# GGN layer of a four-layer graph network: node table as three bf16 pieces, one bf16 matmul of 384 columns per edge tile in place of an f32 one

## The chip, the core and the metric

The kernel runs on one core of one Trainium2 chip. The metric is the device time of one execution in microseconds (us). A core has five engines that run side by side and meet only at semaphores: PE (matmuls; its weight loads are listed as PEld), DVE (vector), ACT (scalar), POOL and SP; DMA queues move data between HBM and on-chip memory. POOL also issues the gathers: indirect DMAs that fetch one table row for each of 128 edges.

## The reference

6250 nodes with 128 features and 100000 edges, sorted by destination, pass four layers: a GAT with two rounds, a GCN, a relational attention layer, and a gated graph layer (GGN). After each, `x = layernorm(x + layer(x))`. The change touches the last layer only:

```python
h = x @ W_in.T + b_in
m = h @ W_msg
agg = jax.ops.segment_sum(m[src], dst, num_segments=n_nodes)
gi = agg @ W_ih.T + b_ih
gh = h @ W_hh.T + b_hh
i_r, i_z, i_n = jnp.split(gi, 3, axis=-1)
h_r, h_z, h_n = jnp.split(gh, 3, axis=-1)
r = jax.nn.sigmoid(i_r + h_r)
z = jax.nn.sigmoid(i_z + h_z)
n = jnp.tanh(i_n + r * h_n)
h_new = (1.0 - z) * n + z * h
return h_new @ W_out.T + b_out
```

The destinations are not spread evenly: an edge's destination is 6250 times the square of a uniform number, so the first blocks of nodes hold the most edges.

## The kernel before, in words

Nodes stand in 49 blocks of 128 (`BLOCKS`), padded to 52 and handled four at a time: 13 quads (`QUADS`). Edges stand in 196 groups (`GROUPS`) of 512, each of four tiles (`GT`) of 128 edges. A visit is one group against one block of destinations; there are 196 + 49 - 1 = 244 visits (`V`), since a group that crosses a block's border is visited again. The whole program is one stage after another, with a barrier between them. Three stages matter here.

**The table stage** (`norm_nodes`, called with the name `ggnt`) takes the sums of the layer ahead, applies the layernorm and writes the table of messages `m` to HBM (`ggn_tab`). It is a pipeline over quads. In turn q of its loop DVE does: the input sums of quad q (L1800, four of L1804), the negative mean (L1702), the reciprocal and offset of quad q-1 (L1705, L1707), and the take of quad q-3 (L1821, in `ggn_take`: the product in PSUM plus a bias, to `ggnt_gsb`). ACT does in its turn q: the squares of quad q (four of L1726, which wait for the mean of quad q), the square root (L1729), and the copy of the transposed quad q-2 (L1734). POOL normalizes a quad (L1744) once its offset is there, PE transposes it (L1755) and multiplies quad q-1 (L1763), SP stores each quad that was taken (L1776). Every engine keeps its own program order.

**The edge stage** (`ggn_edges`) sums table rows by destination. POOL gathers four tiles of 128 rows per group (L265, `gather_group`) into a ring of 14 groups (`SLOTS`), and waits for a slot until PE has made the last visit to the group that lay there (the semaphore `s_o`). SP counts the groups that have landed. DVE makes for each visit four one-hot tiles (L1871, from `iota` and the edge's destination in its block). PE does for each visit four matmuls into one of two PSUM banks (L1954: one-hot times rows; each f32 matmul stands in the trace as two records), after waiting, at every fourth visit, for the group of the visit three ahead. DVE adds the bank to the block's sums (L1879). DVE's order is: one-hots of visit v+1, then the sum of visit v. Ahead of the visits PE and ACT compute `h` and a part of the gates for the 13 quads (L1930, L1937, L1943).

**The gates** (`ggn_gates`) and the last layernorm follow.

The relational layer's table stage (the same `norm_nodes`, under the name `reln`) already cuts a result into three bf16 pieces in `rel_take_dve` and `rel_take_act`: a copy on ACT (L2371), then on DVE a difference (L2378), a cast (L2380) and a difference (L2382). There the pieces of a quad are made one turn late, behind the next quad's take.

## Time and profile before

| what | us |
|---|---|
| three timed runs | 5886.95, 5890.31, 5895.29 |
| their median | 5890.31 |
| span of the profiled execution, first to last instruction | 6933.2 |
| span less median | 1042.9 |

Only the span is shown for the profiled execution; no time of its own around it stands beside it. Its span is 1042.9 us longer than the median of the timed runs, so a difference of two stages in the profile isn't by itself a difference in the time.

A row of a group reads: line, engine, operation, written tile <- read tiles, shapes, count | busy us, mean ns of one | idle time of the engine ahead of them, and what ended most of it. "issue" is a gap in which the engine waited for nothing that the trace shows. In a timeline a row is: start us, duration us, engine, line, operation, tiles, count, and in brackets the idle time before it.

### The profile page before, as it was taken

The page shows a single profiled execution, that of the slowest core. Times are in us where ns is not written, and L with a number is a line of the kernel's source. Part 1 is how long each engine was busy: PE and PEld are TensorE (multiplying, and loading weights), DVE is VectorE, ACT ScalarE, POOL GpSimd, SP SyncE. Part 2 cuts the span into 40 slices and gives each one's busy share as a digit, 9 for nine tenths or more (in the row PEclk, how much of TensorE's full clock was granted, in tenths as well). Part 3 has the DMA queues.
Part 4 walks back from the last instruction along what each step waited for, and adds up shares of the span by engine and source line. Part 5 has one row for each costly group of instructions (what it writes and reads, how often), then busy time and mean ns, then how long its engine had stood idle before and what let it go on. Part 6 is the DMA issues. An engine that isn't in the chain of part 4 may idle for free. (4 is left out here: it accounts for less than half of the span.)

```text
span 6933.2 us, 103287 instructions
## 1 busy us (share of the span) xinstructions
PE 3719.0 (54%) x29332; PEld 3188.5 (46%) x29332; DVE 3593.0 (52%) x11040; ACT 1531.5 (22%) x3908; POOL 3988.6 (58%) x4360
## 2 busy tenths in 40 slices
PE   3555466555434452434454588888885853333436
PEld 1444355544333442334444477777774742223334
DVE  3278655587723343333344577777778951122225
ACT  0255200255300002000000244444442130000003
POOL 6366666266666645666666366666661455666662
PEclk8655577855566676555555799999997976566568
DMA  5266433366522223555564255555553731111111
GB/s 159 88 195 197 141 107 109 95 194 195 165 71 74 73 68 89 137 145 150 157 164 128 72 174 174 175 173 176 174 175 96 205 87 40 47 45 46 45 45 33
DMA packets 511394, 846.13 MB, mean 122 GB/s; under 512 B 116566, under 2 KB 220655, under 8 KB 510271
## 3 DMA queue, kind: packets, MB, share of 16 engines
q0 software_dynamic: 140576, 316.92, 17.7%
q1 hardware_dynamic: 210451, 305.33, 14.5%
q10 hardware_dynamic: 159840, 217.27, 10.8%
q8 instruction: 279, 4.57, 0.3%
q14 instruction: 248, 2.03, 0.1%
HBM read 654.62 MB, written 186.50 MB: 121 GB/s over the span
## 5 line engine op out<-in xcount | busy, mean ns | idle before, releaser
L2456 POOL DMA_INDIRECT s_rows<-rel_tab,src_v x832 | 786.6, 945 | 489.9 <-remote 280.7
L265 POOL DMA_INDIRECT stash<-gat_tab,src_g x784 | 750.9, 958 | 424.3 <-issue 167.4
L265 POOL DMA_INDIRECT gcn_rows<-gcn_tab,src_g x784 | 754.6, 963 | 416.2 <-issue 227.1
L265 POOL DMA_INDIRECT ggn_rows<-ggn_tab,src_g x784 | 744.2, 949 | 413.7 <-issue 224.8
L1621 PE MATMUL e_psb<-tmp,e_oh 128*128 x3328 | 639.7, 362 | 602.0 <-DVE e_oh L1589 391.1
L265 POOL DMA_INDIRECT stash<-in_x,src_g x732 | 705.8, 964 | 385.3 <-issue 154.6
L1621 PEld LDWEIGHTS e_psb<-tmp,e_oh 128*128 128x128 f32 x3328 | 575.2, 262 | 666.9 <-issue 666.4
L1954 PE MATMUL ggn_pso<-ggn_rows,ggn_oh 128*128 x1952 | 389.0, 374 | 693.1 <-issue 273.0
L1169 PE MATMUL g_psc<-g_parts,g_oh 128*128 128x52 bf16 x9408 | 480.5, 222 | 479.5 <-DVE g_oh L1088 260.7
L1954 PEld LDWEIGHTS ggn_pso<-ggn_rows,ggn_oh 128*128 128x128 f32 x1952 | 351.8, 274 | 731.0 <-issue 729.3
L1169 PEld LDWEIGHTS g_psc<-g_parts,g_oh 128*128 128x128 bf16 x9408 | 426.3, 120 | 534.3 <-DVE g_oh L1088 294.6
L2127 PE MATMUL gcn_pso<-gcn_rows,gcn_oh 128*128 x1952 | 452.9, 407 | 153.7 <-issue 84.6
L1879 DVE TENSOR_TENSOR acc<-acc,ggn_pso 128x128 f32 x244 | 70.0, 287 | 895.8 <-DMA tmp<-typev_rows 660.6
L2127 PEld LDWEIGHTS gcn_pso<-gcn_rows,gcn_oh 128*128 128x128 f32 x1952 | 393.8, 300 | 172.9 <-issue 168.7
L2067 DVE TENSOR_TENSOR acc<-acc,gcn_pso 128x128 f32 x244 | 69.8, 286 | 740.9 <-DMA g_lo_rows<-lo_rows 585.9
L1586 DVE COPY tmp<-gx 128x12 f32<-128x12 f32 x392 | 70.5, 180 | 661.3 <-DMA p_early_edges<-in_src 304.0
L2138 PE MATMUL pre_psr<-vt_nv_pieces,tmp 128*128 x832 | 92.5, 182 | 525.5 <-DVE tmp L2080 351.8
L1061 ACT ACTIVATE acc<-g_lo_rows,g_neg_pid 128x512 f32<-128x512 bf16 x392 | 282.9, 722 | 403.3 <-DVE g_oh L1088 225.5
L2138 PEld LDWEIGHTS pre_psr<-vt_nv_pieces,tmp 128*128 128x128 bf16 x832 | 81.2, 114 | 564.1 <-issue 549.6
L1101 DVE TENSOR_TENSOR g_eq<-g_eq,g_psc 128x416 f32<-128x416 f32 x392 | 228.8, 584 | 193.3 <-PE g_psc L1169 144.2
L2485 DVE TENSOR_TENSOR s_psr<-s_psr,s_rows 128x512 f32<-128x512 f32 x208 | 144.8, 696 | 350.2 <-ACT s_psr L2610 301.5
L2610 ACT ACTIVATE s_psr<-s_psr,tm_v 128x128 f32<-128x128 f32 x832 | 230.0, 338 | 417.1 <-remote 379.0
(507 smaller groups left out, 8609.8 us busy)
## 6 DMA issues: line engine op xcount, KB each, us to landing
g_lo_rows<-lo_rows ACTq DMA_DIRECT2D x392, 256.0 KB
oh_dram<-tmp ACTq DMA_DIRECT2D x208, 256.0 KB
s_oh<-oh_dram SPq DMA_DIRECT2D x208, 256.0 KB
edge_v<-acc SPq DMA_DIRECT2D x208, 256.0 KB
r_values<-edge_v SPq DMA_DIRECT2D x208, 256.0 KB, 2.9
edge_v<-stash SPq DMA_DIRECT2D x205, 256.0 KB
e_values<-edge_v SPq DMA_DIRECT2D x205, 256.0 KB
tmp<-drel_rows ACTq DMA_DIRECT2D x208, 128.0 KB
```

Source lines behind the costliest of these rows:

```text
L265: pool.indirect_dma_start(rows[:, t, :], None, tab[:, :], bass.IndirectOffsetOnAxis(ap=edges[:, t:t + 1], axis=0)).then_inc(s_land, 16)
L1061: nc.scalar.activation(sq[:, k % 2, :], trow[:, k, GE:2 * GE], ACT.Square, bias=neg_pid[:, :]).then_inc(s_sq, 1)
L1101: v.tensor_tensor(eq[:, k % 2, :, :, :], eq[:, k % 2, :, :, :], cand, ALU.mult).then_inc(s_take, 1)
L1169: m = nc.tensor.matmul(ps_c[k % 2][:, a * GT + t, 0:NBP], oh[:, k, a * GE + t * P:a * GE + (t + 1) * P], part[:, a, n, :], start=(n == 0), ...
L1586: v.tensor_copy(wv4[:, k, :, D:WCOLS], w.rearrange("p h t -> p t h"))
L1621: nc.tensor.matmul(ps_b[:, bass.ds(bank, 1), 0:WCOLS].rearrange("p o d -> p (o d)"), oh[:, k, t, :], wv[:, bass.ds(slot, 1), :].rearrange( ...
L1954: m = nc.tensor.matmul(ps_o[k % 2][:, 0:D], oh[:, k % 2, t, :], rows[:, bass.ds(slots[k], 1), t, :].rearrange("p o d -> p (o d)"), start=( ...
L2127: m = mm(ps_o[k % 2][:, 0:D], oh[:, k % 2, t, :], rows[:, bass.ds(slots[k], 1), t, :].rearrange("p o d -> p (o d)"), start=(t == 0), stop= ...
L2138: m = mm(ps_n[k % 2][:, t, :], oh2[:, k, t * P:(t + 1) * P], nvp[:, bass.ds(b, 1), :].rearrange("p o n -> p (o n)"), start=True, stop=True)
L2456: pool.indirect_dma_start(rows[:, n % RING, t, :], None, rel_tab[:, :], bass.IndirectOffsetOnAxis(ap=src_v[:, n * GT + t:n * GT + t + 1], ...
L2485: v.tensor_tensor(hm, hm, rows[:, s, :, D:2 * D], ALU.add).then_inc(s_h, 1)
L2610: m = f(ps_r[h][:, t, D:2 * D], ps_r[h][:, t, D:2 * D], ACT.Copy, scale=tm_v[:, bass.ds(n * GT + t, 1)])
```

## The change

The table gets 384 bf16 columns in place of 128 f32 ones: each value is stored as a bf16 number, the bf16 of what is left, and the bf16 of what is then left. A row grows from 512 to 768 bytes. One-hots become bf16, and a tile's sum is one bf16 matmul with 384 columns. DVE adds the three parts of the bank one after another. In the table stage the take of a quad now makes the pieces: DVE adds the bias, ACT copies the first piece, DVE subtracts it, casts the second and subtracts for the third. `w_tab`, `drel_v`, `src_v` and `tm_v` are given back earlier, which makes room for the wider ring; nothing else of the program moves.

```diff
-        ggn_tab = nc.dram_tensor("ggn_tab", (NPAD, D), F32).ap()
+        ggn_tab = nc.dram_tensor("ggn_tab", (NPAD, 3 * D), BF16).ap()
...
+        def ggn_piece(q, i):
+            return pieces[:, q % 2, :, i * D:(i + 1) * D]
+
+        def ggn_take_act(act, q, s_ch, s_eva):
+            act.wait_ge(s_ch, q + 1)
+            nc.scalar.activation(ggn_piece(q, 0), g_rest[:, q % 2, :, :], ACT.Copy).then_inc(s_eva, 1)
+
         def ggn_take(dve, v, q, ps_c, gsb, s_eva, s_ch):
-            return v.tensor_tensor(gsb, ps_c[:, :, 0:D], bias_ggn[:, :].unsqueeze(1).to_broadcast([P, 4, D]), ALU.add)
+            r = g_rest[:, q % 2, :, :]
+            v.tensor_tensor(r, ps_c[:, :, 0:D], bias_ggn[:, :].unsqueeze(1).to_broadcast([P, 4, D]), ALU.add).then_inc(s_ch, 1)
+            if q == 0:
+                v.tensor_copy(iota16[:, :], iota[:, :])
+            dve.wait_ge(s_eva, q + 1)
+            v.tensor_tensor(r, r, ggn_piece(q, 0), ALU.subtract).then_inc(s_gp, 1)
+            dve.wait_ge(s_gp, 2 * q + 1)
+            v.tensor_copy(ggn_piece(q, 1), r).then_inc(s_gp, 1)
+            dve.wait_ge(s_gp, 2 * q + 2)
+            return v.tensor_tensor(ggn_piece(q, 2), r, ggn_piece(q, 1), ALU.subtract)
...
-                rows = sb(st, f"ggn_rows", [P, SLOTS, GT, D])
-                oh = sb(st, f"ggn_oh", [P, 2, GT, P])
+                rows = sb(st, f"ggn_rows", [P, SLOTS, GT, 3 * D], BF16)
+                oh = sb(st, f"ggn_oh", [P, 2, GT, P], BF16)
...
-                                i = v_.tensor_scalar(oh[:, k % 2, t, :], iota[:, :], dst_tab[:, col_], None, ALU.is_equal)
+                                i = v_.tensor_scalar(oh[:, k % 2, t, :], iota16[:, :], dst_tab[:, col_], None, ALU.is_equal)
...
-                            dve.wait_ge(s_acc, v + 2)
                             dve.wait_ge(s_o, v + 1 + RING)
                             ab = acc[:, bass.ds(b * D, D)]
-                            v_.tensor_tensor(ab, ab, ps_o[k % 2][:, 0:D], ALU.add).then_inc(s_acc, 1)
+                            for n in range(3):
+                                dve.wait_ge(s_acc, 3 * v + n + 2)
+                                v_.tensor_tensor(ab, ab, ps_o[k % 2][:, n * D:(n + 1) * D], ALU.add).then_inc(s_acc, 1)
...
-                                pe.wait_ge(s_acc, v + 1)
+                                if v >= 2:
+                                    pe.wait_ge(s_acc, 3 * (v - 1) + 2)
                                 for t in range(GT):
-                                    m = nc.tensor.matmul(ps_o[k % 2][:, 0:D], oh[:, k % 2, t, :], rows[:, bass.ds(slots[k], 1), t, :].rearrange("p o d -> p (o d)"),
+                                    m = nc.tensor.matmul(ps_o[k % 2][:, 0:3 * D], oh[:, k % 2, t, :], rows[:, bass.ds(slots[k], 1), t, :].rearrange("p o d -> p (o d)"),
                                                          start=(t == 0), stop=(t == GT - 1))
...
-        norm_nodes("ggnt", rel_in, w_ggn[:, :], D, [(ggn_tab, None)], None, ggn_take, rel_begin)
+            norm_nodes("ggnt", rel_in, w_ggn[:, :], D, [(ggn_tab, "pieces")], ggn_take_act, ggn_take, rel_begin)
```

On DVE, in the middle of the table stage, one turn of the loop stands in the kernel before like this (input sums, mean, reciprocal, offset, take):

```order
7107 L1800 TENSOR_TENSOR acc<-acc,zrel 128x512
7108 L1804 SCALAR_TENSOR_TENSOR x_n,ggnt_sum<-acc,x_n 128x128 x4
7109 L1702 TENSOR_SCALAR ggnt_minus_mean<-ggnt_sum 128x4
7110 L1705 RECIPROCAL ggnt_sd<-ggnt_sd 128x4
7111 L1707 TENSOR_TENSOR ggnt_off<-ggnt_minus_mean,ggnt_sd 128x4
7112 L1821 TENSOR_TENSOR ggnt_gsb<-ggnt_psc,bias_ggn 128x512
```

and in the changed one like this:

```order
7120 L1805 TENSOR_TENSOR acc<-acc,zrel 128x512
7121 L1809 SCALAR_TENSOR_TENSOR x_n,ggnt_sum<-acc,x_n 128x128 x4
7122 L1704 TENSOR_SCALAR ggnt_minus_mean<-ggnt_sum 128x4
7123 L1707 RECIPROCAL ggnt_sd<-ggnt_sd 128x4
7124 L1709 TENSOR_TENSOR ggnt_off<-ggnt_minus_mean,ggnt_sd 128x4
7125 L1834 TENSOR_TENSOR g_rest<-ggnt_psc,bias_ggn 128x512
7126 L1838 TENSOR_TENSOR g_rest<-g_rest,g_pieces 128x512
7127 L1840 CAST g_pieces<-g_rest 128x4x128
7128 L1842 TENSOR_TENSOR g_pieces<-g_rest,g_pieces 128x4x128
```

The take is now four operations in a row, and the first difference (L1838) reads what ACT has written; the next quad's input sums stand behind all of them.

On ACT the same turn is, in the changed kernel (squares, root, copy of the transposed quad, and the new first piece):

```order
4071 L1728 ACTIVATE ggnt_junk,ggnt_var<-x_n,ggnt_minus_mean 128x128 x4
4072 L1731 ACTIVATE ggnt_sd<-ggnt_var,eps_c 128x4
4073 L1736 ACTIVATE ggnt_xT<-ggnt_psa 128x512
4074 L1830 ACTIVATE g_pieces<-g_rest 128x4x128
4075 L1728 ACTIVATE ggnt_junk,ggnt_var<-x_n,ggnt_minus_mean 128x128 x4
```

The new copy (L1830) stands last in the turn, behind the four squares, which wait for the mean that DVE wrote in this same turn.

In the edge stage DVE's row for one visit (block number, sum, the next one-hots) was in the kernel before:

```order
7560 L1875 TENSOR_LOAD blk_row
7561 L1875 ISA x2
7562 L1879 ISA
7563 L1879 TENSOR_TENSOR acc<-acc,ggn_pso 128x128
7564 L1871 TENSOR_SCALAR ggn_oh<-iota,dst_tab 128x128 x4
```

and is now:

```order
7567 L1896 TENSOR_LOAD blk_row
7568 L1896 ISA x2
7569 L1901 ISA
7570 L1901 TENSOR_TENSOR acc<-acc,ggn_pso 128x128 x3
7571 L1892 TENSOR_SCALAR ggn_oh<-iota,dst_tab 128x128 x4
```

One sum became three; the one-hots keep their place and count.

## Rows read from the trace of the kernel before

**Rows 1.** The page, costliest groups: the five large gathers of the program.

```profile
L2456 POOL DMA_INDIRECT s_rows<-rel_tab,src_v x832 | 786.6, 945 | 489.9 <-remote 280.7
L265 POOL DMA_INDIRECT stash<-gat_tab,src_g x784 | 750.9, 958 | 424.3 <-issue 167.4
L265 POOL DMA_INDIRECT gcn_rows<-gcn_tab,src_g x784 | 754.6, 963 | 416.2 <-issue 227.1
L265 POOL DMA_INDIRECT ggn_rows<-ggn_tab,src_g x784 | 744.2, 949 | 413.7 <-issue 224.8
L265 POOL DMA_INDIRECT stash<-in_x,src_g x732 | 705.8, 964 | 385.3 <-issue 154.6
```

**Rows 2.** Instructions on the ring `ggn_rows`: ns min/median/max, first and last start.

```profile
L1954 PE MATMUL ggn_pso<-ggn_rows,ggn_oh x1952: 274/421/578, 5751.8 to 6833.3; 128*128 x196
L265 POOL DMA_INDIRECT ggn_rows<-ggn_tab,src_g x784: 938/944/1325, 5660.2 to 6809.0; - x196
```

**Rows 3.** Timeline inside the edge stage: POOL's gathers, and one wait of POOL and DVE.

```profile
5783.10 0.94 POOL L265 DMA_INDIRECT ggn_rows<-ggn_tab,src_g  x1 [0.31 <-issue]
5784.35 0.94 POOL L265 DMA_INDIRECT ggn_rows<-ggn_tab,src_g  x1 [0.30 <-issue]
5787.82 0.29 DVE L1879 TENSOR_TENSOR acc<-acc,ggn_pso 128x128 f32 x1 [6.71 <-DMA tmp<-typev_rows]
5788.39 0.94 POOL L265 DMA_INDIRECT ggn_rows<-ggn_tab,src_g  x1 [3.09 <-DMA tmp<-typev_rows]
```

**Rows 4.** Busy time by stretch of 100 us (PE, PEld, DVE, ACT, POOL; PEclk, DMA share, GB/s).

```profile
6460.00:6560.00 100.00, 42.74 (x192) 37.95 (x192) 30.01 (x126) 0.00 (x0) 65.36 (x68) 0.58 0.18 45
```

**Rows 5.** Timeline of DVE, the last visits of the edge stage.

```profile
6830.19 0.29 DVE L1879 TENSOR_TENSOR acc<-acc,ggn_pso 128x128 f32 x1 [0.67 <-PE ggn_pso L1954]
6830.39 0.87 DVE L1871 TENSOR_SCALAR ggn_oh<-iota,dst_tab 128x128 f32<-128x128 f32 x4
6831.18 0.28 DVE L1879 TENSOR_TENSOR acc<-acc,ggn_pso 128x128 f32 x1
...
6832.77 0.29 DVE L1879 TENSOR_TENSOR acc<-acc,ggn_pso 128x128 f32 x1 [0.53 <-PE ggn_pso L1954]
```

**Rows 6.** The takes of the table stage: ns min/median/max, first and last start, waits.

```profile
L1821 DVE TENSOR_TENSOR ggnt_gsb<-ggnt_psc,bias_ggn x13: 684/692/692, 5612.4 to 5655.5; 128x512 f32<-128x512 f32 x13
...
  PE ggnt_psc L1763: 16.9, 8
```

**Rows 7.** Timeline of DVE in the table stage: first take, and means of quads 4 and 12.

```profile
5612.42 0.69 DVE L1821 TENSOR_TENSOR ggnt_gsb<-ggnt_psc,bias_ggn 128x512 f32<-128x512 f32 x1 [2.91 <-PE ggnt_psc L1763]
5613.03 0.68 DVE L1800 TENSOR_TENSOR acc<-acc,zrel 128x512 f32<-128x512 f32 x1
...
5614.71 0.17 DVE L1702 TENSOR_SCALAR ggnt_minus_mean<-ggnt_sum 128x4 f32<-128x4 f32 x1
...
5647.62 0.17 DVE L1702 TENSOR_SCALAR ggnt_minus_mean<-ggnt_sum 128x4 f32<-128x4 f32 x1
...
5650.05 0.16 DVE L1707 TENSOR_TENSOR ggnt_off<-ggnt_minus_mean,ggnt_sd 128x4 f32<-128x4 f32 x1
...
5654.55 0.69 DVE L1821 TENSOR_TENSOR ggnt_gsb<-ggnt_psc,bias_ggn 128x512 f32<-128x512 f32 x1 [1.53 <-PE ggnt_psc L1763]
```

**Rows 8.** Timeline of DVE in the `reln` table stage: the pieces of one quad.

```profile
3904.38 0.68 DVE L2378 TENSOR_TENSOR q_rest<-q_rest,acc 128x512 f32<-128x512 f32 x1
3905.09 0.43 DVE L2380 CAST tmp<-q_rest 128x512 bf16<-128x512 f32 x1
3905.55 0.69 DVE L2382 TENSOR_TENSOR tmp<-q_rest,tmp 128x512 bf16<-128x512 f32 x1
3906.16 0.68 DVE L2392 TENSOR_TENSOR reln_gsb<-reln_psc,w_b 128x512 f32<-128x512 f32 x1
```

**Rows 9.** The next turn there: DVE's mean, then ACT's squares to first piece.

```profile
3907.97 0.17 DVE L1702 TENSOR_SCALAR reln_minus_mean<-reln_sum 128x4 f32<-128x4 f32 x1
3908.17 0.40 ACT L1726 ACTIVATE reln_junk<-x_n,reln_minus_mean 128x128 f32<-128x128 f32 x1 [3.05 <-DVE reln_minus_mean L1702]
...
3910.53 0.62 ACT L2371 ACTIVATE acc<-q_rest 128x512 bf16<-128x512 f32 x1
```

**Rows 10.** The page: time from issue to landing of a table store, the last number.

```profile
ggn_tab<-ggnt_gsb SPq DMA_DIRECT2D x13, 256.0 KB, 2.3
```

**Rows 11.** Groups of one shape: bf16 operations elsewhere in the program.

```profile
L2079 DVE TENSOR_SCALAR tmp<-tmp,vt_pid 128x512 bf16<-128x512 bf16 x208 | 75.3, 362 | 1.8 <-DMA tmp<-typev_rows 1.0 <-issue 0.8
L2546 PE MATMUL s_psr<-rel_hm,s_oh 128*128 128x256 bf16 x832 | 195.6, 275 | 16.8 <-DMA s_oh<-oh_dram 12.8 <-issue 3.9
L2574 PE MATMUL s_psk<-bkp,ones 128*128 128x512 bf16 x208 | 79.3, 381 | 38.2 <-issue 33.0 <-DVE tmp L2510 5.2
```

More of the change, by code:

```diff
@@ L126, in build @@
         iota = sb(top, "iota", [P, P])
+        iota16 = sb(top, "iota16", [P, P], BF16)
         x_n = sb(top, "x_n", [P, NBP * D])
@@ L130, in build @@
         dst_tab = sb(top, "dst_tab", [P, VP * GT])
-        w_tab = sb(top, "w_tab", [P, VP * GT])
         blk_row = sb(top, "blk_row", [1, VP], I32)
@@ L138, in build @@
         done_row = sb(top, "done_row", [1, GROUPS], I32)
-        drel_v = sb(top, "drel_v", [P, VT])
-        src_v = sb(top, "src_v", [P, VT], I32)
-        tm_v = sb(top, "tm_v", [P, VT])
         blkv_row = sb(top, "blkv_row", [1, VT], I32)
@@ L286, in keep_rows @@
                 keep_store(sp, l, j)
+        visits = ExitStack()
+        w_tab = sb(visits, "w_tab", [P, VP * GT])
+        drel_v = sb(visits, "drel_v", [P, VT])
+        src_v = sb(visits, "src_v", [P, VT], I32)
+        tm_v = sb(visits, "tm_v", [P, VT])
         gat = ExitStack()
@@ L1774, in _ @@
                             for tab, source in stores:
-                                src = gsb[:, q % 2, :, :] if source is None else qd(source, q).rearrange("p (j d) -> p j d", d=D)
+                                if source == "pieces":
+                                    src = pieces[:, q % 2, :, :]
+                                else:
+                                    src = gsb[:, q % 2, :, :] if source is None else qd(source, q).rearrange("p (j d) -> p j d", d=D)
                                 sp.dma_start(tab[q * 4 * P:(q + 1) * 4 * P, :].rearrange("(j p) c -> p j c", p=P), src).then_inc(s_st[q % 2], 16)
@@ L1902, in _ @@
                         back(V - 1, (V - 1) % RING)
-                        dve.wait_ge(s_acc, V + 2)
+                        dve.wait_ge(s_acc, 3 * V + 2)
                     @block.scalar
@@ L2783, in build @@
         rel_sums()
-        norm_nodes("ggnt", rel_in, w_ggn[:, :], D, [(ggn_tab, None)], None, ggn_take, rel_begin)
+        with ExitStack() as spare:
+            g_rest = sb(spare, "g_rest", [P, 2, 4, D])
+            pieces = sb(spare, "g_pieces", [P, 2, 4, 3 * D], BF16)
+            s_gp = top.enter_context(nc.semaphore("g_pieces_made"))
+            norm_nodes("ggnt", rel_in, w_ggn[:, :], D, [(ggn_tab, "pieces")], ggn_take_act, ggn_take, rel_begin)
         rel.close()
+        visits.close()
         hb = sb(top, "ggn_candidate", [P, NBP * D])
```

## The prediction

> **What bounds the kernel now.** I read the page's costliest groups first. The five large gathers [rows 1] look alike: a gather takes POOL 945 to 964 ns, and an idle time stands beside it in the same proportion everywhere. The timeline shows how this comes about [rows 3]: gathers start 1.25 us apart (0.94 us of work, 0.30 us of gap), and now and then POOL stops for some us and goes on together with DVE, on an event that the trace doesn't show. In the edge stage of the GGN the 784 gathers run from 5660.2 to 6809.0 [rows 2], and the stage's matmuls end 25 us later. At their own pace they would need 784 x 1.247 = 978 us; they took 1150.
>
> Who then sets the pace of that stage? Not PE: its 192 records in 100 us are 24 visits (8 records each), and they keep it busy 43 us; DVE is busy 30 us, while POOL issues 68 gathers, 17 groups, and is busy 65 us [rows 4]. With a gap of 0.30 us per gather that is 85 us of POOL's 100. So POOL is the engine at work, and PE and DVE follow it.
>
> The missing 15% are the joint stops. They matter, because the profiled span is 1042.9 us longer than the median of the timed runs. Taking 0.31 us per gather off the idle times of [rows 1] leaves 232, 181, 173, 171 and 158 us, together 915 us. That is close to the whole difference, so I take it that timed runs gather at about 1.247 us without the stops, and that the edge stage lasts there some 978 us plus its last visits. This is an inference; a rival below lives on its being wrong.
>
> The table stage ahead of it is bound otherwise. Its 13 takes go from 5612.4 to 5655.5, DVE waiting only 16.9 us for PE in it [rows 6]: DVE, ACT, POOL and PE hand each quad around, with nothing large that could cover an added step, and the gathers can't begin before its last store has landed.
>
> **The change part by part.**
>
> *PE in the edge stage.* A matmul of 384 bf16 columns lies between the bf16 ones of 256 (275 ns) and 512 columns (381 ns) [rows 11], by interpolation 328 ns, against two records of 421 ns (median) [rows 2]. Records of a stream overlap, so I take about 1.3 us for four of them, where a visit's eight records took 1.1 to 2.1 us. PE has 4.0 us per visit (978 / 244). Worth nothing on the path.
>
> *Gathers.* A row grows from 512 to 768 bytes. The relational gathers fetch 1024-byte rows at 945 ns against 949 here [rows 1], so issuing doesn't depend on the row's size. The DMA engines are busy 18% [rows 4]; half as many bytes again makes some 27%. Zero.
>
> *DVE in the edge stage.* Unhindered, a visit costs DVE 0.99 us, from one sum to the next [rows 5]. Two sums are added. Each waits for the one before: at least 0.29 us, and with a semaphore between (0.71 us start to start for a 0.68 us operation, [rows 8]) 0.33 us; at most 0.5 us, the sum's 0.29 us plus the 0.2 us by which any next operation follows it here. One-hots get cheaper: 512 bf16 columns take 362 ns [rows 11], where four of 128 f32 columns take 0.87 us, so between nothing and 0.5 us. A visit then costs 1.15 to 2.0 us; I take 1.9, since the four short one-hots stay four instructions. In the busiest part there are 24 visits to 17 groups, 1.4 a group, so 2.7 us of DVE in the 5.0 us that POOL needs for a group. Hidden by the gathers. Were that cover gone, 244 x 0.9 = 220 us would show.
>
> *Last visits.* Behind the last landing there are four visits. Before they go in pairs of 2.6 us at the fast clock (6830.19 to 6832.77, [rows 5]) and slower at the other, the first two starting at once: about 8.5 us. After, DVE's 1.9 us rules: 1.5 + 4 x 1.6 to 1.9, about 8 us. I put -0.6, with +-3.
>
> *The table stage.* This is the term that counts. ACT's new copy stands behind the four squares of the same turn, and these wait for the mean that DVE has just written; DVE then stands still until the copy is there, makes the pieces, and only then begins the next quad's sums, on which the next mean depends. So the turn becomes a closed loop through both engines:
> - from DVE's mean to the end of ACT's copy: 3910.53 + 0.62 - 3907.97 = 3.18 us, and about 0.1 us to reach DVE [rows 9];
> - difference, cast, difference, until the next operation starts: 3906.16 - 3904.38 = 1.78 us [rows 8];
> - the next quad's input sums until its mean: 5614.71 - 5613.03 = 1.68 us [rows 7].
>
> That makes 6.74, with hand-overs 6.8 us a turn. Now eight turns, from the mean of quad 4 to that of quad 12, take 5647.62 - 5614.71 = 32.9 us [rows 7], 4.1 each; then they take 54.4: **+21.5 us**. In the turn of the first take ACT is free: bias add 0.69, copy 0.62, pieces 1.78 and the small cast of `iota` come to 3.3 us until the next sums instead of 0.61: **+2.7**. Behind the mean of quad 12 the stage needs 5655.5 + 0.7 - 5647.6 = 8.5 us now [rows 6, 7]. Then: 5.1 for the take of quad 9; 0.35 to the offset of quad 12; 4.5 from an offset to the product one quad back (5650.05 to 5654.55, [rows 7]), which covers the take of quad 10; and two takes of 3.2 us for quads 11 and 12. Together 16.3: **+7.8**. Sum of the stage: **+32.0 us**.
>
> Bounds: the DVE work alone is 13 x 1.78 = 23.1 us, and if it filled DVE's 16.9 us of waits [rows 6] it would cost 6; if no part of a turn overlapped with anything it would cost 13 x (3.3 + 1.78) = 66. The loop's hand-overs leave +-5 around 32.
>
> *Stores.* 384 KB a quad in place of 256, landing 2.3 us after issue [rows 10]. Only the last counts: 0 to +1.2 (in proportion), +0.6 taken. Room in memory and the released tables: nothing.
>
> Sum: 32.0 + 0.6 - 0.6 = **+32 us**. Against the profiled execution that is 6933.2 + 32 = 6965 if the joint stops stay as they are; against the timed median, 5890.3 + 32 = **5922 us**.
>
> Two rules of the Trainium skill bear on this. The page "SBUF — State Buffer", section "Who interferes with whom", says that a VectorE cast or tensor-scalar operation in a two-port mode keeps GpSimd off the port pair that it also uses to write its DMA descriptors, for the whole instruction. By that rule shorter one-hots would free the gathers; the row bounds it: mean 949 ns against a median of 944, so 784 x 5 ns = 4 us at most, and the sum would be +28. The other, "VectorE: DVE Perf Modes", section "The DRAIN you can't avoid", says that each VectorE operation pays its own pipeline flush, chained or not, and so speaks against three sums in place of one; the sums are priced above from rows and lie hidden.
>
> **The rivals.**
>
> *A. The stops are partly real in timed runs, and the change relieves them: faster.* For it: POOL and DVE restart together on something that hangs on PE [rows 3], and PE's records fall by half. Against it: the 915 us. If 40% of this stage's 171 us were real and went away, the time would be 32 - 68 = -36: 5854 us. It decides from 45 us of stops removed in timed runs. 0.10.
>
> *B. The pieces fill waits in the table stage: no change that can be measured.* 23.1 - 16.9 = +6: 5896 us. For it: DVE waits every other turn now. Against it: ACT's program order puts the copy behind the squares of the same turn. It needs the copy to be ready about when the bias add is done. 0.11.
>
> *C. DVE falls behind in the edge stage: much slower.* It needs a visit of over 3.5 us in the busy part (5.0 / 1.4), or a backlog like that of the profile at the end: 25 us of visits at 1.3 us would be 36 at 1.9, so +11 on top, 5933; fully bound by DVE, over 6000. Against it: 1.9 us. 0.03 for the large one.
>
> The forecast itself: 0.76, its own range 5911 to 5934.
>
> **How the numbers follow.** A measurement of this kernel tells changes over about 0.2%, 12 us. Faster is A, 0.10; same is B with a little of the forecast's lower edge, 0.12; slower 0.78. The range leaves out A and the large C and takes in B and the smaller backlog of C: 5895 to 5942.
>
> **What would show it.** In the changed trace: takes about 6.8 us apart in the middle of the table stage, 13 of them from first to last start over some 72 us instead of 43; DVE waiting there for ACT's copy, some 2 us a turn; gathers still 1.25 us apart; PE's busy time in the edge stage well below 389 us. A stage between 48 and 55 us would be B. POOL waiting for PE and DVE's sums with no stop of the joint kind, or over 3.5 us between sums in a burst, would be C. The profiled span itself may even fall, if the stops of a profiled run shrink with the number of records; a fall there together with slower timed runs would bear out the reading of the 1042.9 us, and timed runs that are faster would make it wrong.

## The result, and the profile after

| | us |
|---|---|
| before, median of 4 runs (lowest to highest) | 5892.8 (5887.0 to 5897.3) |
| after, median of 4 runs (lowest to highest) | 5920.9 (5920.1 to 5924.6) |
| after : before, 95% interval | 1.0053 [1.0039, 1.0067] |
| span of the profiled execution of after | 5919.9 |

The changed kernel is 0.5% slower: 28.1 us by these medians, where 32 were predicted. Its profiled span agrees with its timed runs to 1 us. The stops of [rows 3] are gone, and not from the changed stage alone.

The page of the changed kernel, the groups that answer to [rows 1]:

```profile
L2479 POOL DMA_INDIRECT s_rows<-rel_tab,src_v x832 | 787.6, 947 | 271.0 <-issue 252.6
...
L262 POOL DMA_INDIRECT ggn_rows<-ggn_tab,src_g x784 | 745.0, 950 | 252.9 <-issue 234.9
...
L262 POOL DMA_INDIRECT stash<-in_x,src_g x732 | 708.6, 968 | 223.7 <-issue 146.1
```

A gather costs what it did. Four of the five stages of [rows 1] were not touched, and their idle times fell as well (489.9 to 271.0 for the first), so the stops say nothing about the change.

Instructions on the ring `ggn_rows`, answering to [rows 2], with what POOL's gathers waited for and the landing time:

```profile
L1977 PE MATMUL ggn_pso<-ggn_rows,ggn_oh x976: 326/524/528, 4854.8 to 5817.0; 128*128 x196
L262 POOL DMA_INDIRECT ggn_rows<-ggn_tab,src_g x784: 942/947/1462, 4824.8 to 5807.4; - x196
...
  POOL ggn_rows L262: 3.7, 12
DMA to landing us min/median/max: 2.5/2.6/4.1
```

The gathers go from 4824.8 to 5807.4, 1.255 us apart on average, and in the whole stage POOL waited 3.7 us for PE. Rows of 768 bytes land in 2.6 us. The stretch that answers to [rows 4]:

```profile
5460.00:5560.00 100.00, 30.13 (x97) 12.18 (x98) 41.38 (x183) 0.00 (x0) 75.93 (x80) 0.59 0.28 78
```

POOL issues 80 gathers in these 100 us and is the engine at work; PE is busy 30 us, DVE 41. The DMA engines are busy 28%, where 27 were expected.

The takes of the table stage, answering to [rows 6]:

```profile
L1834 DVE TENSOR_TENSOR g_rest<-ggnt_psc,bias_ggn x13: 683/691/693, 4744.3 to 4816.6; 128x512 f32<-128x512 f32 x13
...
  PE ggnt_psc L1765: 4.8, 2
```

They take 72.3 us from first to last start, where [rows 6] had 43.1. One turn, first on DVE and then on ACT:

```profile
4762.60 0.17 DVE L1704 TENSOR_SCALAR ggnt_minus_mean<-ggnt_sum 128x4 f32<-128x4 f32 x1
...
4762.96 0.69 DVE L1834 TENSOR_TENSOR g_rest<-ggnt_psc,bias_ggn 128x512 f32<-128x512 f32 x1
4765.81 0.69 DVE L1838 TENSOR_TENSOR g_rest<-g_rest,g_pieces 128x512 f32<-128x512 f32 x1 [2.16 <-ACT g_pieces L1830]
4766.54 0.43 DVE L1840 CAST g_pieces<-g_rest 128x512 bf16<-128x512 f32 x1
4767.00 0.69 DVE L1842 TENSOR_TENSOR g_pieces<-g_rest,g_pieces 128x512 bf16<-128x512 f32 x1
4767.61 0.68 DVE L1805 TENSOR_TENSOR acc<-acc,zrel 128x512 f32<-128x512 f32 x1
...
4769.30 0.17 DVE L1704 TENSOR_SCALAR ggnt_minus_mean<-ggnt_sum 128x4 f32<-128x4 f32 x1
```

```profile
4762.80 0.40 ACT L1728 ACTIVATE ggnt_junk<-x_n,ggnt_minus_mean 128x128 f32<-128x128 f32 x1 [3.72 <-DVE ggnt_minus_mean L1704]
...
4764.68 0.58 ACT L1736 ACTIVATE ggnt_xT<-ggnt_psa 128x512 f32<-128x512 f32 x1
4765.16 0.62 ACT L1830 ACTIVATE g_pieces<-g_rest 128x512 bf16<-128x512 f32 x1
```

The bias add ends at 4763.65, but ACT is in the squares, which it began after the mean of 4762.60; the root and the copy to `xT` follow, and the first piece is ready only at 4765.78. DVE stands still for 2.16 us and the turn is 6.70 us. The loop's parts are 3.2 us from the mean to the first difference, 1.80 for the pieces and 1.69 for the next quad's sums.

The last visits, on DVE, answering to [rows 5]:

```profile
5813.27 0.93 DVE L1901 TENSOR_TENSOR acc<-acc,ggn_pso 128x128 f32 x3 [9.88 <-PE ggn_pso L1977]
5814.12 0.73 DVE L1892 TENSOR_SCALAR ggn_oh<-iota,dst_tab 128x128 bf16<-128x128 bf16 x4
5814.77 0.92 DVE L1901 TENSOR_TENSOR acc<-acc,ggn_pso 128x128 f32 x3
5815.61 0.73 DVE L1892 TENSOR_SCALAR ggn_oh<-iota,dst_tab 128x128 bf16<-128x128 bf16 x4
5816.26 0.92 DVE L1901 TENSOR_TENSOR acc<-acc,ggn_pso 128x128 f32 x3
```

An unhindered visit is 1.49 us: 0.85 us from the first of three sums to the one-hots, 0.65 from these to the next sum.

### The profile page after: what moved, and what is told of

Same layout as the page of the kernel before. It is cut to its first block and busy times, and to the rows that moved or that the text cites. A ratio compares the mean times of both kernels' runs of the same rounds, so it can differ in the third digit from the quotient of the medians.

```text
span 5919.9 us, 101771 instructions
## 1 busy us (share of the span) xinstructions
PE 3354.0 (57%) x28252; PEld 2842.6 (48%) x28356; DVE 3708.7 (63%) x11568; ACT 1541.7 (26%) x3921; POOL 3989.9 (67%) x4360
## 5 line engine op out<-in xcount | busy, mean ns | idle before, releaser
L2479 POOL DMA_INDIRECT s_rows<-rel_tab,src_v x832 | 787.6, 947 | 271.0 <-issue 252.6
L262 POOL DMA_INDIRECT ggn_rows<-ggn_tab,src_g x784 | 745.0, 950 | 252.9 <-issue 234.9
L2150 PE MATMUL gcn_pso<-gcn_rows,gcn_oh 128*128 x1952 | 407.1, 378 | 532.4 <-SPq L972 521.1
L1977 PE MATMUL ggn_pso<-ggn_rows,ggn_oh 128*128 x976 | 300.4, 466 | 662.5 <-SPq L972 604.0
L2150 PEld LDWEIGHTS gcn_pso<-gcn_rows,gcn_oh 128*128 128x128 f32 x1952 | 356.7, 275 | 549.2 <-issue 548.0
L1901 DVE TENSOR_TENSOR acc<-acc,ggn_pso 128x128 f32 x732 | 208.9, 285 | 619.4 <-PE ggn_pso L1977 601.6
L1977 PEld LDWEIGHTS ggn_pso<-ggn_rows,ggn_oh 128*128 128x128 bf16 x976 | 121.1, 124 | 842.3 <-issue 824.4
L1591 DVE TENSOR_TENSOR e_oh<-e_psi,drel_v 128x512 f32<-128x512 f32 x416 | 284.0, 683 | 22.3 <-PE e_psb L1623 22.3
L2724 POOL COPY r_wv<-score 128x32 f32<-128x32 f32 x208 | 107.9, 519 | 267.6 <-PE r_psb L2768 158.6
L1636 ACT ACTIVATE acc<-e_psb 128x128 f32<-128x128 f32 x98 | 27.2, 278 | 989.9 <-PE e_psb L1623 989.9
L2599 PE MATMUL s_psk<-w_kv,s_msgT 128*128 128x128 f32 x1664 | 219.7, 275 | 110.8 <-DVE tmp L2533 110.5
L2082 DVE TENSOR_SCALAR gcn_oh<-iota,dst_tab,w_tab 128x128 f32<-128x128 f32 x976 | 274.9, 363 | 0.0
```

What stands on the lines that cost most here:

```text
L262: pool.indirect_dma_start(rows[:, t, :], None, tab[:, :], bass.IndirectOffsetOnAxis(ap=edges[:, t:t + 1], axis=0)).then_inc(s_land, 16)
L1591: v.tensor_tensor(oh[:, k % RING, :, :], iota_p.unsqueeze(1).to_broadcast([P, GT, P]), drel_v[:, bass.ds(n * GT, GT)].unsqueeze(2).to_broa ...
L1901: v_.tensor_tensor(ab, ab, ps_o[k % 2][:, n * D:(n + 1) * D], ALU.add).then_inc(s_acc, 1)
L1977: m = nc.tensor.matmul(ps_o[k % 2][:, 0:3 * D], oh[:, k % 2, t, :], rows[:, bass.ds(slots[k], 1), t, :].rearrange("p o d -> p (o d)"), sta ...
L2082: i = v.tensor_scalar(oh[:, k % 2, t, :], iota[:, :], dst_tab[:, col_], w_tab[:, col_], ALU.is_equal, ALU.mult)
L2150: m = mm(ps_o[k % 2][:, 0:D], oh[:, k % 2, t, :], rows[:, bass.ds(slots[k], 1), t, :].rearrange("p o d -> p (o d)"), start=(t == 0), stop= ...
```

## The experiments

Each kernel was timed beside the kernel before on the same chip, but the sets of runs stand on different chips, so two experiments are compared by what each lies above its own runs of before, and by their traces. The changed kernel lies 28.1 us above before in the first set of runs and 35.5 in the second, which is told at the end of this section. "Stage" below is the time from the table stage's first mean to the first gather, read from the trace.

### The kernel before, once more

No edit.

> The kernel before, unchanged, profiled once more. Theory (the joint stops belonged to that one profiled execution and not to the kernel): the new profile has a span within 10 us of the timed runs, about 5890 us, the 784 gathers of the GGN's edge stage start 1.25 us apart and the stage takes about 980 us instead of 1150, and the 13 takes of the table stage still go over some 43 us. Rival (the kernel of before has the stops whenever it is profiled, and the change took them away): a span of some 6930 us again, with gathers' idle time near 490 us.

Measured: 5886.6 us against 5885.9, ratio 1.0002 [0.9993, 1.0011]; the profiled span is 5881.4 us. Its page, and the instructions on the ring and the takes:

```profile
L265 POOL DMA_INDIRECT ggn_rows<-ggn_tab,src_g x784 | 744.0, 949 | 246.8 <-issue 233.1
```

```profile
L265 POOL DMA_INDIRECT ggn_rows<-ggn_tab,src_g x784: 940/944/1351, 4789.5 to 5771.2; - x196
```

```profile
L1821 DVE TENSOR_TENSOR ggnt_gsb<-ggnt_psc,bias_ggn x13: 682/691/692, 4742.1 to 4784.8; 128x512 f32<-128x512 f32 x13
```

The same kernel, without the stops: 246.8 us of idle time before this stage's gathers instead of 413.7, and 1229 instead of 2129 before all five groups of [rows 1]; gathers over 981.7 us instead of 1149, takes over 42.7. The 1042.9 us of the first profile belonged to that one execution. From here on this profile stands for before.

### The edge stage alone, and the table stage alone

In the first, two pieces stay zero, so that it computes with a table rounded to bf16; ACT has no part in the take:

```diff
-            r = g_rest[:, q % 2, :, :]
-            v.tensor_tensor(r, ps_c[:, :, 0:D], bias_ggn[:, :].unsqueeze(1).to_broadcast([P, 4, D]), ALU.add).then_inc(s_ch, 1)
             if q == 0:
                 v.tensor_copy(iota16[:, :], iota[:, :])
...
-            return v.tensor_tensor(ggn_piece(q, 2), r, ggn_piece(q, 1), ALU.subtract)
+                v.memset(pieces[:, :, :, D:3 * D], 0.0)
+            return v.tensor_tensor(ggn_piece(q, 0), ps_c[:, :, 0:D], bias_ggn[:, :].unsqueeze(1).to_broadcast([P, 4, D]), ALU.add)
```

> The edge stage of the change alone: the table is stored as bf16 rows of 384, but the table stage writes only the first piece (one add that writes bf16) and leaves the other two at zero, so the sums are those of a table rounded to bf16. Theory (all of the loss is in the table stage, the edge stage is bound by the gathers' issue in both kernels): within 0.1% of before, 5887 to 5895 us; first to last take about 43 us. Rival 1 (the edge stage gains a little, which hides part of a larger loss): 5880 to 5886. Rival 2 (the two extra sums or the larger rows cost something in the edge stage): over 5897, up to 5920 if the loss is there.

Measured: 5888.6 us against 5885.9, ratio 1.0000 [0.9991, 1.0009]. The takes cover 43.8 us.

The second is the kernel before, with the pieces made beside its f32 table:

```diff
-            return v.tensor_tensor(gsb, ps_c[:, :, 0:D], bias_ggn[:, :].unsqueeze(1).to_broadcast([P, 4, D]), ALU.add)
...
+            v.tensor_tensor(s, ps_c[:, :, 0:D], bias_ggn[:, :].unsqueeze(1).to_broadcast([P, 4, D]), ALU.add).then_inc(s_ch, 1)
+            if q == 0:
+                v.tensor_copy(iota16[:, :], iota[:, :])
+            dve.wait_ge(s_eva, q + 1)
+            v.tensor_tensor(r, s, ggn_piece(q, 0), ALU.subtract).then_inc(s_gp, 1)
+            dve.wait_ge(s_gp, 2 * q + 1)
+            v.tensor_copy(ggn_piece(q, 1), r).then_inc(s_gp, 1)
+            dve.wait_ge(s_gp, 2 * q + 2)
+            return v.tensor_tensor(ggn_piece(q, 2), r, ggn_piece(q, 1), ALU.subtract)
```

> The table stage of the change alone: the three pieces are made as in the change, by the same operations and waits, but the f32 table is stored and the f32 edge stage of before follows; the pieces are used by nobody. Theory: the whole loss appears, 5917 to 5926 us, with turns of 6.7 us and 13 takes over 72 us. Rival (the loss is in the edge stage): within 3 us of before, 5890.

Measured: 5917.1 us against 5885.9, ratio 1.0051 [1.0037, 1.0065]. The takes of this kernel:

```profile
L1833 DVE TENSOR_TENSOR g_sum<-ggnt_psc,bias_ggn x13: 683/691/693, 4744.7 to 4817.0; 128x512 f32<-128x512 f32 x13
```

72.3 us again. The two halves of the change add up to the whole: from the edge stage nothing that the timed runs can tell (their interval is 5 us to either side), 31 us from the table stage.

### Pieces made one turn later

```diff
+                            if q >= 4 and late is not None:
+                                late(dve, v, q - 4, s_eva)
                             if q >= 3:
                                 dve.wait_ge(s_mm, q - 2)
...
-                            sp.wait_ge(s_evd, q + 1)
+                            if late is None:
+                                sp.wait_ge(s_evd, q + 1)
+                            else:
+                                sp.wait_ge(s_gp, 3 * (q + 1))
```

> The changed kernel with one thing moved: a quad's two differences and the cast are made one turn later, after the next offset, so that DVE no longer waits for ACT's copy of the same turn. Same operations, same edge stage. Theory (the turn of 6.7 us is a closed loop through ACT's squares and copy): the turn becomes DVE's own work, 1.7 (sums and mean) + 0.4 (reciprocal, offset) + 1.8 (pieces) + 0.7 (bias add) = 4.6 to 4.9 us, eight turns give back 14 to 17 us and the tail 1 to 4: 5901 to 5907 us. Rival (the added DVE work itself is what costs, not the waiting): DVE's work is the same, so 5917 to 5923.

Measured: 5899.6 us against 5885.9, ratio 1.0024 [1.0014, 1.0035]. It lies 13.7 us above before, where the changed kernel lies 28 to 36 above it and the pieces alone 31.2 on this same chip: 14 to 22 us of the loss are given back. By the traces it is 18.7, and the time is a little better than expected. One turn on DVE, and POOL beside it:

```profile
4763.52 0.17 DVE L1704 TENSOR_SCALAR ggnt_minus_mean<-ggnt_sum 128x4 f32<-128x4 f32 x1
...
4763.89 0.68 DVE L1852 TENSOR_TENSOR g_rest<-g_rest,g_pieces 128x512 f32<-128x512 f32 x1
4764.61 0.57 DVE L1854 CAST g_pieces<-g_rest 128x512 bf16<-128x512 f32 x1
4765.21 0.82 DVE L1856 TENSOR_TENSOR g_pieces<-g_rest,g_pieces 128x512 bf16<-128x512 f32 x1
4765.95 0.68 DVE L1844 TENSOR_TENSOR g_rest<-ggnt_psc,bias_ggn 128x512 f32<-128x512 f32 x1
4766.55 0.76 DVE L1813 TENSOR_TENSOR acc<-acc,zrel 128x512 f32<-128x512 f32 x1
...
4768.32 0.17 DVE L1704 TENSOR_SCALAR ggnt_minus_mean<-ggnt_sum 128x4 f32<-128x4 f32 x1
```

```profile
4764.07 2.71 POOL L1751 TENSOR_SCALAR x_n<-x_n,ggnt_sd,ggnt_off 128x128 f32<-128x128 f32 x4 [2.09 <-DVE ggnt_off L1709]
```

No wait is left on DVE in these turns, and the turn is 4.80 us, DVE's own work. So 1.9 us of the 2.6 us that each turn had gained were waiting and 0.7 us are work; of these 0.7 us, 0.27 are the cast and the last difference, which take longer beside POOL's scaling than in the changed kernel (0.57 and 0.82 us instead of 0.43 and 0.69). From the mean of quad 4 to that of quad 12 it takes 38.5 us instead of 53.6 (before: 32.5), and the whole stage 72.7 instead of 91.4 (before: 59.3). The tail gave back only 1.0 us, the low end of what was expected: with no sums left to stand between, each of the last takes still waits for its own copy (0.69 to 0.70 us, as in the changed kernel's tail below).

### ACT's copy ahead of its squares

```diff
+                            first = name == "ggnt" and 3 <= q < QUADS
+                            if first:
+                                take_act(act, q - 3, s_ch, s_eva)
                             if q < QUADS:
                                 act.wait_ge(s_nm, q + 1)
```

> The changed kernel with ACT's order changed in the table stage alone: from the fourth turn to the thirteenth the copy of the first piece stands ahead of the four squares, not behind them. Theory (DVE's wait of 2.2 us a turn is for squares that stand ahead of the copy): the copy is there about 0.7 us after the bias add, the turn becomes 1.7 + 0.4 + 0.7 + 0.7 + 1.8 = 5.3 us, ten turns of which eight in full give back 11 to 14 us: 5907 to 5910 us. Rival (the squares, moved behind, hold up reciprocal and offset, and the loop is as long as before by another way round): turn 6.3 to 6.8, 5917 to 5923 us.

> The kernel with ACT's copy ahead of the squares, once more, on the chip of the changed kernel. Its first profile has turns of 5.87 us and takes over 64.9 us in place of 72.3, but its timed median lay only 3.6 us below that of the changed kernel, in another set of runs. Theory (turns of 0.83 us less, 7 us in all, are real): 6 to 9 us below the changed kernel's median here. Rival (nothing is gained in timed runs): within 3 us of it.

Measured: 5917.3 us against 5888.2 (ratio 1.0052 [1.0038, 1.0065]), and the second time 5912.8 us beside 5920.6 of the changed kernel on the same chip (ratio 1.0048 [1.0035, 1.0062] to 5885.1). The gain is about half of what was first expected: a turn is 5.87 us, not 5.3. The 6 to 9 us expected of the second run came as 7.8. DVE in the first of the two profiles:

```profile
4765.08 0.69 DVE L1837 TENSOR_TENSOR g_rest<-ggnt_psc,bias_ggn 128x512 f32<-128x512 f32 x1 [0.56 <-PE ggnt_psc L1768]
4766.47 0.69 DVE L1841 TENSOR_TENSOR g_rest<-g_rest,g_pieces 128x512 f32<-128x512 f32 x1 [0.70 <-ACT g_pieces L1833]
```

The wait for the copy fell from 2.16 to 0.70 us as expected, but a new one of 0.56 us stands before the bias add. ACT's squares, and behind them its copy of `xT`, are now later, and PE's product with them. What stands ahead of the copy on ACT (the squares, the root and the copy of `xT`) is thus shown to be what DVE waits for; moving it only shortens the loop from 6.70 to 5.87 us. The second profile has a stage of 85.2 us against 91.4, 6.2 us less. In the first set of runs the timings show no gain (29.0 us above its own before, where the changed kernel was 28.1 above its own); on one chip all five runs (5911.9 to 5918.3 us) lie below the five of the changed kernel (5918.9 to 5924.0). The intervals of the ratios, 8 us to either side, could not tell the gain from none; the traces can.

### The first piece cast on DVE

```diff
+            dve.wait_ge(s_ch, q + 1)
+            v.tensor_copy(ggn_piece(q, 0), r).then_inc(s_eva, 1)
             dve.wait_ge(s_eva, q + 1)
```

> The changed kernel with the first piece cast by DVE itself in place of ACT's copy: one more DVE operation a turn, and no hand-over to ACT and back. Theory (the waiting costs, 2.2 us a turn; the cast costs 0.4 to 0.6): turn 4.9 to 5.2 us, 12 to 15 us given back in eight turns and 0 to 3 at the end: 5903 to 5909 us. Rival (DVE's own work bounds the turn): DVE has more of it, so 5925 us or more.

Measured: 5912.7 us against 5888.2, ratio 1.0044 [1.0030, 1.0058]. More work on DVE, and yet not slower than the changed kernel: its turns are 5.3 and 5.8 us by turns, 5.51 on average. The rival is out, but the gain is smaller than expected: eight turns give back 9.5 us where 12 to 15 were expected, the stage 11.4 (80.0 instead of 91.4), and by what each lies above its own before it is 4 to 11. In each turn two of DVE's four operations on the pieces were longer than the ones they were priced by, and these lie beside POOL's scaling (4763.21 to 4765.83 in this turn):

```profile
4764.94 0.57 DVE L1842 CAST g_pieces<-g_rest 128x512 bf16<-128x512 f32 x1
4765.54 0.82 DVE L1844 TENSOR_TENSOR g_pieces<-g_rest,g_pieces 128x512 bf16<-128x512 f32 x1
```

0.57 and 0.82 us, where the same two take 0.43 and 0.69 in the changed kernel.

### More sums in the edge stage

Nine and twelve chained sums a visit instead of three; those past the third go to a tile that nothing reads.

```diff
-                            for n in range(3):
-                                dve.wait_ge(s_acc, 3 * v + n + 2)
-                                v_.tensor_tensor(ab, ab, ps_o[k % 2][:, n * D:(n + 1) * D], ALU.add).then_inc(s_acc, 1)
+                            for n in range(9):
+                                dve.wait_ge(s_acc, 9 * v + n + 2)
+                                to = ab if n < 3 else more[:, :]
+                                v_.tensor_tensor(to, to, ps_o[k % 2][:, n % 3 * D:(n % 3 + 1) * D], ALU.add).then_inc(s_acc, 1)
```

> The changed kernel with nine chained sums a visit instead of three in the edge stage; the six added ones go to a tile that nobody reads. Nothing else is changed. Theory (DVE's sums lie hidden under the issue of the gathers): a visit costs DVE 1.5 + 6 x 0.32 = 3.4 us where the gathers give 4.0, so the stage stays at 984 us, and only the four visits behind the last gather show, 4 x 1.9 = 8 us: 5927 to 5933 us, with a few us more if bursts of visits overrun. Rival (sums are on the path, the two added ones too): 244 x 1.9 = 470 us slower.

Measured: 5932.9 us against 5888.2, ratio 1.0076 [1.0060, 1.0091]. The 1464 added sums of 0.29 us are 420 us of work. By the traces, from the stage's first mean to the end, they cost 11.6 us over the changed kernel, 8.8 of these behind the last gather, where 8 were expected.

> As the one with nine sums, with twelve: a visit costs DVE 1.5 + 9 x 0.32 = 4.4 us, more than the 4.0 that the gathers give. Theory (the cover ends at about 4.0 us a visit): the stage becomes 244 x 4.4 = 1070 us, 80 to 100 us slower than the changed kernel, 6000 to 6020 us; gathers wait for PE's sums. Rival (DVE isn't what would take over, PE's visit grows with it or the sums overlap): under 5945 us.

Measured: 6056.8 us against 5888.2, ratio 1.0287 [1.0271, 1.0303]: 133 to 140 us over the changed kernel, above what was expected. The stretch of [rows 4] in the kernel with nine sums, and then in that with twelve; under it the ring of the latter:

```profile
5460.00:5560.00 100.00, 37.83 (x109) 13.92 (x109) 88.29 (x349) 0.00 (x0) 75.93 (x80) 0.52 0.29 78
```

```profile
5460.00:5560.00 100.00, 32.09 (x88) 11.17 (x88) 90.91 (x356) 0.00 (x0) 75.80 (x80) 0.50 0.29 79
```

```profile
L1980 PE MATMUL ggn_pso<-ggn_rows,ggn_oh x976: 326/527/528, 4860.2 to 5947.9; 128*128 x196
L262 POOL DMA_INDIRECT ggn_rows<-ggn_tab,src_g x784: 941/947/1264, 4830.3 to 5864.8; - x196
...
  POOL ggn_rows L262: 60.2, 32
```

With nine sums DVE is busy 88 of 100 us and the gathers hardly notice: first to last they take 983.7 us instead of 981.8. With twelve, this stretch still holds 80 gathers, but DVE falls behind over the stage: POOL waits 60.2 us for PE in it, the gathers take 1034.5 us, and the visits run on for 83 us behind the last one. A visit takes 4.39 us, 5902.86 to 5907.25 for instance, and 244 x 4.39 = 1071 us from PE's first visit on would be DVE's pace; 1087.7 were measured. The expectation was too low, since it counted the 1070 us from the first gather; PE begins 30 us after it. So the cover holds at 3.4 us a visit and is gone at 4.4; the changed kernel needs 1.5.

### The changed kernel again, and the third piece on POOL

> The changed kernel unchanged, timed once more beside the runs of the same chip. Theory: slower than before by 28 to 32 us again (ratio 1.0045 to 1.0055), 13 takes over 72 us, turns of 6.70 us. It is the measure for the two runs beside it.

Measured: 5920.6 us against 5885.1, ratio 1.0061 [1.0047, 1.0074]; a turn is 6.70 us. The ratio is a little above the range that was expected. Taken together the two comparisons put the change at 28 to 36 us.

> The kernel with pieces made a turn later, with the second difference (the third piece) on POOL instead of DVE, behind POOL's scaling of the same turn, and three buffers of pieces instead of two. Theory (with the waits gone, the turn is DVE's own work): DVE has 0.7 us less a turn, so the turn goes from 4.80 to 4.1 to 4.3 us, about the turn of the kernel before; 8 turns give 4 to 5.5 us, and the tail may lose 1 to 2 for a slower operation on POOL: 5895 to 5899 us, within 0.2% of before and not below it. Rival (POOL's difference takes over 2.5 us, so that scaling and difference fill POOL's turn, or holds up DVE): 5900 us or more.

This is the kernel with the late pieces, with the last difference given to POOL; the edit is shown against the changed kernel.

```diff
-            return v.tensor_tensor(ggn_piece(q, 2), r, ggn_piece(q, 1), ALU.subtract)
...
+        def ggn_last(pool, q):
+            pool.wait_ge(s_gp, 2 * q + 2)
+            nc.gpsimd.tensor_tensor(ggn_piece(q, 2), g_rest[:, q % 2, :, :], ggn_piece(q, 1), ALU.subtract).then_inc(s_gq, 1)
```

Measured: 5939.8 us against 5885.1, ratio 1.0092 [1.0076, 1.0107]: some 40 us slower than with the piece on DVE (54.7 above its own before instead of 13.7). The theory is out. The rival's "5900 or more" holds the number, and POOL's difference does hold up DVE (it takes 1.19 us, not over 2.5), but that explains only the stage, 1.4 us longer than with the late pieces; the rest nobody expected. POOL in the table stage, DVE beside it, and then two groups of gathers, the first of which ends some 2600 us before the first added operation:

```profile
4782.56 2.70 POOL L1752 TENSOR_SCALAR x_n<-x_n,ggnt_sd,ggnt_off 128x128 f32<-128x128 f32 x4 [1.16 <-DVE ggnt_off L1710]
4785.23 1.19 POOL L1864 TENSOR_TENSOR g_pieces<-g_rest,g_pieces 128x512 bf16<-128x512 f32 x1
```

```profile
4785.32 1.24 DVE L1823 SCALAR_TENSOR_TENSOR x_n<-acc,x_n 128x128 f32<-128x128 f32 x1
...
4786.49 0.28 DVE L1823 SCALAR_TENSOR_TENSOR x_n<-acc,x_n 128x128 f32<-128x128 f32 x1
```

```profile
L262 POOL DMA_INDIRECT stash<-gat_tab,src_g x784: 951/955/2740, 1113.3 to 2112.1; - x196
L262 POOL DMA_INDIRECT ggn_rows<-ggn_tab,src_g x784: 952/957/1402, 4836.8 to 5825.9; - x196
```

The turn became 5.02 us instead of 4.80, so taking the difference from DVE gained nothing in the stage: while POOL makes it, one of DVE's input sums takes 1.24 us instead of 0.28, turn after turn, which is more than the 0.74 us that the difference had cost DVE. And a gather costs 11 ns more (medians 955 and 957 ns; 944 and 946 in the changed kernel on the same chip): the five large groups of gathers together are busy 38 us longer. Of the 39.5 us between this profile and that with the late pieces, 32.6 lie ahead of the stage's first mean and 7.6 between the first and the last gather of the edge stage. Why is open: most of these gathers run long before the new operation, so it is not contention with it.

## Why the prediction was right

By its own steps, with the new profile of before (5881.4 us) against the second one of the changed kernel (5919.0 us):

| | before | after | difference | predicted |
|---|---|---|---|---|
| start to the stage's first mean | 4730.2 | 4733.4 | +3.2 | 0 |
| mean of quad 0 to that of quad 4 | 14.2 | 16.7 | +2.6 | +2.7 |
| mean of quad 4 to that of quad 12 | 32.5 | 53.6 | +21.1 | +21.5 |
| mean of quad 12 to the first gather | 12.6 | 21.1 | +8.5 | +7.8 +0.6 |
| first gather to last gather | 981.7 | 981.8 | +0.1 | 0 |
| last gather to the end | 110.2 | 112.4 | +2.2 | -0.6 |

*The table stage.* The stage gains 32.1 us, and 32.6 were predicted with the store. The loop was priced at 6.8 us a turn and is 6.70; 3.2, 1.8 and 1.7 us are its parts, as they were read from [rows 7 to 9]. It is a closed loop through ACT's squares and copy: the kernel with late pieces takes out the wait and gets 18.7 us back in the stage, with the same operations. What remains, 13.7 us in the timed runs and 13.4 in the stage's rows, lies in DVE's own work (6.0 us in the eight turns) and in the tail (7.5). The last takes of the changed kernel, from its second profile:

```profile
4813.23 0.69 DVE L1834 TENSOR_TENSOR g_rest<-ggnt_psc,bias_ggn 128x512 f32<-128x512 f32 x1 [0.80 <-PE ggnt_psc L1765]
4814.61 0.69 DVE L1838 TENSOR_TENSOR g_rest<-g_rest,g_pieces 128x512 f32<-128x512 f32 x1 [0.70 <-ACT g_pieces L1830]
...
4816.41 0.68 DVE L1834 TENSOR_TENSOR g_rest<-ggnt_psc,bias_ggn 128x512 f32<-128x512 f32 x1
```

3.2 us a take, as predicted. From the mean of quad 12 (4803.7) to the end of the last piece (4819.7) it is 16.0 us; 16.3 were predicted. From there to the first gather it is 5.1 us, where before it was 4.0: the wider store and the start cost 1.1 us, and 0.6 were put down.

*The edge stage.* The gathers' pace was read as POOL's own, 978 us for 784, and is 982 in both kernels. PE's busy time on the ring fell from 377 us to 300 and 310 in the two profiles and was worth nothing, as was said: the edge stage alone gives 1.0000. The matmul itself was priced too low: 328 ns by interpolation is what the shortest take (326), but the median is 524 to 527 ns, in a stretch with a granted clock of about 0.6. The cost of DVE's visit was put at 1.9 us, near the upper of its bounds, and is 1.49; that term was mis-sized, but lies hidden. The sums follow each other by 0.32 us (0.33 predicted). With two more sums at 0.33 us and one-hots at their old price the visit of 0.99 us would have become 1.65, so 0.25 of the 1.9 had no row behind it; the rest of the error is the one-hots, which in bf16 take 0.65 us until the next sum instead of 0.79. The two bounds, 1.15 and 2.0, held it. By the rule of the Trainium skill's page "VectorE: DVE Perf Modes", section "The DRAIN you can't avoid", each chained sum pays its own flush. The traces go with it as far as they reach: no sum starts before the one ahead has ended, 0.29 us each and 0.32 us from start to start in the kernels with three, nine and twelve. But each sum here also waits for a semaphore of the one ahead, so no run shows the flush by itself.

*The last visits.* -0.6 was predicted, with 3 us to either side, and it is +2.2. Up to the next stage's first transposes it is +1.0 (12.0 us behind the last gather before, 13.0 after): PE ends its four visits at the same distance, 10.6 us, and the last sums, three instead of one, take 0.93 us instead of 0.29. So the term had the wrong sign: DVE's 1.9 us a visit did not rule there, PE's visits got no shorter, and the next stage, at +1.2 us, was put at nothing. Both fit a difference in the clock. First the trace of before, then that of after, the 13 us of the last visits and the 20 us behind them (columns as in [rows 4]):

```profile
5771.00:5784.00 13.00, 7.09 (x37) 6.64 (x38) 2.72 (x12) 0.09 (x1) 0.94 (x1) 0.65 0.12 12
5784.00:5804.00 20.00, 20.00 (x69) 10.34 (x68) 11.90 (x25) 10.90 (x16) 0.00 (x0) 1.00 0.00 1
```

```profile
5807.00:5820.00 13.00, 6.07 (x18) 2.58 (x19) 4.66 (x20) 0.00 (x0) 0.57 (x1) 0.50 0.17 16
5820.00:5840.00 20.00, 20.00 (x68) 10.67 (x67) 10.73 (x24) 9.62 (x14) 0.00 (x0) 0.92 0.00 1
```

In this trace PE comes out of the changed edge stage at a granted clock of 0.50, the lower of its two levels (1.2 of 2.4 GHz), where before it was 0.65 on average. A visit of four matmuls takes 1.4 us there, and the next stage's first pairs of products 1.92 and 1.48 us instead of 1.02. The first profile of the changed kernel has 0.72 in the last visits, and PE is done 9.9 us behind the last gather, so the low clock in the visits themselves is not there every time. What all traces share is the start of the next stage: in the 20 us behind the visits the eight profiles with the bf16 edge stage and three sums show 0.85 to 0.94, and 111.8 to 113.9 us from the last gather to the end; the two with the f32 edge stage (before, profiled again, and the table stage alone) show 1.00, and 110.2 and 109.3 us. So the 2 us come with the new edge stage, which the kernel with the edge stage alone shows too (112.6 us); that the clock is their cause is argued from these rows and not tested by a run that changes the clock by itself.

*The stops.* The inference from the 1042.9 us was right: the same kernel of before, profiled again, has none of them. Rival A, which lived on their being partly real, is out; the rows that it leaned on name a DMA and not PE as what ended the stop [rows 3]. *Rival B* is out: takes over 72 us. DVE's waits for PE's products did go, 16.6 us before and 4.8 after, but 22.1 us of waits for ACT's copy came in their place, which is what B needed not to happen. *Rival C* needed visits of over 3.5 us; the runs with more sums show that this bound was placed well, between 3.4 and 4.4.

*The other rule.* The page "SBUF — State Buffer" of the Trainium skill, section "Who interferes with whom", would have had the shorter bf16 one-hots free the gathers, by the prediction's rows up to 4 us. The median gather went from 944 to 946 ns and the mean stayed at 949, so nothing was freed, and the trace doesn't bear the rule out here.

*The total.* 28.1 us in the first comparison and 35.5 in the second, each uncertain by 8; 32 was predicted, and the traces say 32.1 + 0.1 + 2.2 = 34. The sum was not saved by errors that cancel: the large term is within 1 us, and the small one that went wrong, the last visits, is 2.8 us off, inside the 3 us that it was given. The 3.2 us ahead of the stage are scatter: over all these profiles the first mean comes between 4730.0 and 4738.3, though the kernels don't differ up to there (that with a piece on POOL apart).

## What to carry to other kernels

Work that is added between two engines costs the loop that it closes, not its own duration: follow one quad's hand-overs around, through every engine's program order, before pricing an added step, and place a hand-over so that a full turn lies between the order and the use. Making a stage's PE work a fifth cheaper is worth nothing where the pace is that of another engine's issue; what was paid for it in the stage ahead is nearly the whole result (32 us of 34). If a profiled span is far above the timed runs, price every stage by its undisturbed rows and look for the surplus in stages that the change doesn't touch.
